# The order of the engines' steps in the first half of a two-part transformer kernel, written out anew

## The reference

```python
q, k, v = (out @ W[l] + b[l] for each of Wq, Wk, Wv)      # 16 heads of 16
Qf, Kf = favor(q), favor(k)     # [exp(u - h), exp(-u - h)], u = x @ omega, h = |x|^2 / 2
a = causal_linear_attention(Qf, Kf, v)   # running sums of Kf and of Kf v, num / den
h = layer_norm(out + a @ Wo[l] + bo[l])
out = layer_norm(h + relu(h @ W1[l] + bf1[l]) @ W2[l] + bf2[l])
```

## Time and profile before

| | |
|---|---|
| median of 3 runs | 2771.56 us (2768.94 to 2773.91) |
| the profiled execution's own time | 2766.34 us |
| its span in the profile | 2764.5 us |
| TensorE, VectorE, ScalarE, GpSimd busy | 95%, 81%, 55%, 53% |
| mean granted TensorE clock | 0.99 |
| chunks' passes of the first half in the span | chunk 0 from 20 us on, the last to about 1360 us |

### The profile page before, as it was taken

The page is one execution under the profiler, slowest core; times in us unless marked ns, Lnnn a source line. Parts: engine busy times, 40 slices in busy tenths (PEclk is TensorE's granted clock), DMA queues, the critical chain, the costliest instruction groups (busy, mean ns, idle before and its releaser), DMA issues.

```text
span 2764.5 us, 61451 instructions
## 1 busy us (share of the span) xinstructions
PE 2632.8 (95%) x21416; PEld 2141.0 (77%) x21416; DVE 2228.9 (81%) x5246; ACT 1516.8 (55%) x3106; POOL 1457.5 (53%) x1406
## 2 busy tenths in 40 slices
PE   6799999999999999999988899999999999999997
PEld 4578878778878887787776688888878778788876
DVE  7678877787677777888899988888888888888875
ACT  3454445444554455444435766777756666666661
POOL 2344344443343445444566766665666666676653
PEclk9999999999999999999999999999999999999999
DMA  3100000010000000000111100000100100101001
GB/s 101 28 9 9 17 2 17 9 38 2 1 1 7 19 26 16 21 17 24 45 46 47 32 10 17 14 17 14 32 29 26 34 16 29 32 29 32 18 26 44
DMA packets 77731, 65.63 MB, mean 24 GB/s; under 512 B 15394, under 2 KB 72698, under 8 KB 77434
## 3 DMA queue, kind: packets, MB, share of 16 engines
q1 hardware_dynamic: 77434, 61.70, 7.4%
HBM read 49.10 MB, written 12.58 MB: 22 GB/s over the span
## 4 chain that ended last, share of the span: by engine, by line
PE 58%; DVE 21%; ACT 10%; issue 8%; POOL 2%; DMA 0%; SPq 0%; DVEq 0%; ACTq 0%; POOLq 0%
PE PS L273 49%; DVE U L1575 3%; PE PS L778 3%; DVE X L1448 2%; DVE ZC L1646 2%; ACT U L1069 2%; ACT U L1070 2%; ACT U L1071 2%; DVE ST L1429 2%; ACT U L1072 1%; DVE Z L1440 1%; ACT FB L1096 1%; PE PS L731 1%; PE PS L740 1%; DVE Z L1528 1%
## 5 line engine op out<-in xcount | busy, mean ns | idle before, releaser
L1251 ACT ACTIVATE PR<-PS,SM 128x256 f32<-128x256 f32 (+1 forms) x512 | 279.4, 555 | 101.9 <-DVE SM L1767 100.4
L1096 ACT ACTIVATE FB<-PS,BC 128x512 f32<-128x512 f32 x192 | 132.4, 689 | 293.2 <-PE PS L273 290.7
L2159 POOL TENSOR_TENSOR RL<-FB,RH 128x512 fp32r<-128x512 f32 x96 | 124.1, 1293 | 277.2 <-DVE RH L1553 277.2
L1575 DVE TENSOR_TENSOR U<-PS,CST 128x512 f32<-128x512 f32 x384 | 236.4, 677 | 24.1 <-PE PS L273 24.1
L1762 DVE CUSTOM_DVE_ANT_0 PS<-PS,MSK 128x256 f32<-128x256 f32 (+1 forms) x512 | 202.6, 436 | 46.6 <-PE PS L273 45.3
L1104 ACT COPY NUM<-PS 128x256 f32<-128x256 f32 x96 | 35.8, 373 | 353.7 <-DVE TMP L1567 304.1
L273 PE MATMUL PS<-W2H,RH 128*128 128x256 f32 x768 | 222.6, 290 | 4.4 <-DVE RL L1556 3.8
L1553 DVE CAST RH<-FB 128x512 fp32r<-128x512 f32 x192 | 87.8, 457 | 171.2 <-ACT FB L1096 167.6
L2284 POOL TENSOR_TENSOR SM<-SM,COL 128x8 f32<-128x8 f32 x128 | 215.0, 1679 | 10.7
L273 PE MATMUL PS<-W2H,RL 128*128 128x256 f32 x768 | 215.8, 281 | 0.0
L273 PE MATMUL PS<-W2L,RH 128*128 128x256 f32 x768 | 215.3, 280 | 0.0
(11 more groups left out here) (266 smaller groups left out, 8995.1 us busy)
## 6 DMA issues: line engine op xcount, KB each, us to landing
PX<-in_L_attn_x SPq DMA_DIRECT2D x16, 512.0 KB, 4.0
TB<-in_k_rot SPq DMA_DIRECT2D x64, 128.0 KB, 2.1
SG<-in_L_attn_W SPq DMA_DIRECT2D x24, 256.0 KB, 2.7
xp_scratch<-PX SPq DMA_DIRECT2D x8, 512.0 KB, 2.9
xs_scratch<-X SPq DMA_DIRECT2D x64, 64.0 KB, 1.5
ZS<-xs_scratch SPq DMA_DIRECT2D x16, 256.0 KB, 2.9
GG<-xp_scratch SPq DMA_DIRECT2D x7, 512.0 KB, 3.7
out<-GG SPq DMA_DIRECT2D x7, 512.0 KB, 3.7
```

Source lines behind the costliest of these rows:

```text
L1096: e.activation(FB[:, hb % 2, :], PS[:, 5, :], ACT.Relu, bias=BC[:, l % 2, 4 + hb:5 + hb]).then_inc(*a_re.up(n, hb))
L1251: t = e.activation(PR[:, par, 256 * i + lo:256 * i + hi], PS[:, 3 + par, 256 * i + lo:256 * i + hi], ACT.Exp, bias=S[:, 40 + 2 * g + i:41 ...
L1575: e.tensor_tensor(heads(U[:, u % 6, :], 4), heads(PS[:, g, :], 4), bcast(CM, 4), ALU.mult).then_inc(*d_mk.up(n, u))
L2159: e.tensor_tensor(RL[:, r, :], FB[:, 0, :], RH[:, r, :].bitcast(F), ALU.subtract).then_inc(*p_rl.up(n, hb))
```

## The change

No product, mask or norm is added or left out. Four things change.

1. **Laps 2 to 23** get a new order on all four engines. On TensorE the four `favor` stand in one run; `down` 0 and 1 stand ahead of them, `down` 2 to 7 among scores and sums and at the end, three of them behind `scores(n, 3)`; `scores(n, 0)` stands ahead of `key_sums`. VectorE's norms are cut into statistics (`_s`) and centring (`_c`): the first norm's centring lies between `state(n, 0)` and `masks(n, 1)`, its scaling ahead of `masks(n, 3)`. GpSimd's `key_state(n, 0)` lies ahead of `low_hidden(m, 4)`. Each step stays in the lap in which it was.
2. **Laps 0 and 1** and what stands ahead of them are written out step by step. Two modulation products stand ahead of `turn_x(0)`, four among chunk 0's `values` and `favor`, the last two in banks 5 and 6. The splits of the first twelve weight pieces, the gates' rows and the prologues of chunks 2 and 3 have new places.
3. ScalarE copies all six modulation products and adds the 1 in the same step (an activation with bias `ONE`); VectorE's copy and three additions are gone.
4. `k_col`, `k_cst` and the three other constants have semaphores of their own; `k_col` is sent third, the modulation's weights ahead of x, `load_columns(0)` ahead of the last three constants. Waits that stood in the loops stand in the steps' functions.

The new order of TensorE in the opening and in the laps, then ScalarE's, VectorE's (opening's begin and laps) and GpSimd's laps:

```diff
-    MODS = [(0, 0, 4), (1, 0, 5), (0, 1, 6), (1, 1, 7), (0, 2, 0), (1, 2, 1)]
+    MODS = [(0, 0, 4), (1, 0, 5), (0, 1, 6), (1, 1, 7), (0, 2, 5), (1, 2, 6)]
...
+        modulate(0)
+        modulate(1)
         turn_x(0)
+        proj(0, 0)
+        proj(0, 1)
+        proj(0, 2)
+        proj(0, 3)
+        values(0, 0)
+        modulate(2)
+        values(0, 1)
+        modulate(3)
+        favor(0, 0, 2)
+        modulate(4)
+        favor(0, 1, 3)
+        modulate(5)
+        favor(0, 2, 0)
+        favor(0, 3, 1)
...
+        for n in range(2, 24):
+            w, m = n - 1, n - 2
+            up(m, 0)
+            spread(w)
+            up(m, 1)
+            proj(n, 0)
+            proj(n, 1)
+            up(m, 2)
+            proj(n, 2)
+            proj(n, 3)
+            values(n, 0)
+            values(n, 1)
+            down(m, 0)
+            down(m, 1)
+            favor(n, 0, 2)
+            favor(n, 1, 3)
+            favor(n, 2, 0)
+            favor(n, 3, 1)
+            up(m, 3)
+            attn_out(w, 0)
+            attn_out(w, 1)
+            turn_k(n, 0)
+            turn_k(n, 1)
+            up(m, 4)
+            scores(n, 0)
+            key_sums(n)
+            up(m, 5)
+            down(m, 2)
+            sums(n, 0)
+            scores(n, 1)
+            down(m, 3)
+            up(m, 6)
+            sums(n, 1)
+            scores(n, 2)
+            up(m, 7)
+            down(m, 4)
+            sums(n, 2)
+            scores(n, 3)
+            down(m, 5)
+            down(m, 6)
+            down(m, 7)
+            turn_h(w)
+            if n < 23: turn_x(n + 1)
+            sums(n, 3)
...
+            if j == 0:
+                e.activation(MOD[:, b, D:2 * D], PS[:, bank, 256:512], ACT.Identity, bias=ONE)
+                t = e.copy(MOD[:, b, 0:D], PS[:, bank, 0:256])
...
+        for n in range(2, 24):
+            w, m = n - 1, n - 2
+            numerators(w, 3)
+            relu(m, 0)
+            relu(m, 1)
+            operands(n, 0)
+            operands(n, 1)
+            operands(n, 2)
+            operands(n, 3)
+            attention(w, 0)
+            attention(w, 1)
+            relu(m, 2)
+            features(n, 0, 2)
+            features(n, 1, 3)
+            features(n, 2, 0)
+            relu(m, 3)
+            features(n, 3, 1)
+            keep_rows(n, 0)
+            keep_rows(n, 1)
+            relu(m, 4)
+            relu(m, 5)
+            numerators(n, 0)
+            relu(m, 6)
+            relu(m, 7)
+            numerators(n, 1)
+            numerators(n, 2)
+            high_mid(w, 0)
+            high_mid(w, 1)
+            if n < 23: high_row(n + 1, 0)
+            if n < 23: high_row(n + 1, 1)
...
+        clear_values()
+        silu()
         prologue(0)
+        modulate_a(0)
+        modulate_b(0)
         split(0)
         split(1)
+        lower(0, 0, 2, 0, a_x, d_x)
+        lower(0, 1, 3, 0, a_x, d_x)
         split(2)
         prologue(1)
+        split(3)
+        add_bv(0, 0)
         modulate_a(1)
+        split(4)
         modulate_b(1)
+        add_bv(0, 1)
+        running(0, 0)
+        running(0, 1)
+        prologue(2)
+        carry(0)
+        split(5)
+        split(6)
+        masks(0, 0)
+        normaliser(0)
+        state(0, 0)
+        masks(0, 1)
...
+        for n in range(2, 24):
+            w, m, z = n - 1, n - 2, n - 3
+            scale_num(w, 0)
+            scale_num(w, 1)
+            rounded(m, 0)
+            if z >= 0: add_down(z)
+            if z >= 0: norm2_s(z)
             splits(n, "a")
+            rounded(m, 1)
+            if z >= 0: norm2_c(z)
+            add_bv(n, 0)
             splits(n, "v")
+            add_bv(n, 1)
+            if z >= 0: norm2_b(z)
+            running(n, 0)
+            rounded(m, 2)
+            running(n, 1)
+            carry(n)
+            rounded(m, 3)
+            add_wo(w)
+            norm1_s(w)
+            rounded(m, 4)
+            masks(n, 0)
+            normaliser(n)
+            rounded(m, 5)
+            state(n, 0)
+            norm1_c(w)
+            masks(n, 1)
+            rounded(m, 6)
+            if z in CH3: norm3_s(z)
+            if n < 6: prologue(n + 2)
             splits(n, "m0")
+            state(n, 1)
             splits(n, "m1")
+            masks(n, 2)
+            rounded(m, 7)
+            state(n, 2)
+            norm1_b(w)
+            masks(n, 3)
+            if z in CH3: norm3_c(z)
+            if n < 6: modulate_a(n + 2)
+            lower(w, 0, 0, 1, a_h, d_h)
+            lower(w, 1, 1, 1, a_h, d_h)
+            if n < 23: lower(n + 1, 0, 2, 0, a_x, d_x)
+            if n < 23: lower(n + 1, 1, 3, 0, a_x, d_x)
+            state(n, 3)
+            if n < 6: modulate_b(n + 2)
+            if z in CH3: norm3_b(z)
             splits(n, "m2")
...
+        for n in range(2, 24):
+            w, m, z = n - 1, n - 2, n - 3
+            if n == 19: gate_rows(0)
+            if z in CH3: add_bias(z)
+            if n in (2, 11): features_of(1 if n == 2 else 2)
+            add_bf2(m)
+            if z >= 0: rsqrt(("2", z))
+            low_hidden(m, 0)
             splits(n, "a")
+            if n == 19: gate_rows(1)
+            low_attention(w, 0)
+            low_attention(w, 1)
+            low_hidden(m, 2)
+            scale_queries(n, 0)
+            scale_queries(n, 1)
+            key_state(n, 0)
+            low_hidden(m, 4)
+            add_bo(n)
+            splits(n, "m0")
+            rsqrt(("1", w))
+            key_state(n, 1)
             splits(n, "v")
+            low_hidden(m, 6)
             splits(n, "m1")
+            if z in CH3: rsqrt(("3", z))
+            key_state(n, 2)
+            if n < 6: rsqrt(("p", n + 2))
+            key_state(n, 3)
             splits(n, "m2")
...
+        e.dma_start(COL[:, :], ins["k_col"]).then_inc(*s_col.up())
```

More of the change, by code:

```diff
@@ L480, in scores @@
         def scores(n, j):
+            if j == 0:
+                for i in range(2):
+                    e.wait_ge(*a_kt.at(n, i))
+                    if n > 0:
+                        e.wait_ge(*d_z.at(n - 1, i))
+                    else:
+                        e.wait_ge(*a_fe.at(n, i))
             for m in range(2):
@@ L538, in up @@
                     e.wait_ge(*d_h.at(n, k))
+            if n == 0 and hb == 0:
+                e.wait_ge(*a_mod.at(5))
             if hb or n:
@@ new lines, in _ @@
+        proj(0, 0)
[12 more added lines that the diff above has]
+        favor(0, 3, 1)
+        turn_k(0, 0)
+        turn_k(0, 1)
+        scores(0, 0)
+        key_sums(0)
+        scores(0, 1)
+        sums(0, 0)
+        sums(0, 1)
+        scores(0, 2)
+        sums(0, 2)
+        scores(0, 3)
@@ new lines, in _ @@
+        turn_x(1)
+        sums(0, 3)
+        spread(0)
+        proj(1, 0)
+        proj(1, 1)
+        proj(1, 2)
+        proj(1, 3)
+        values(1, 0)
+        values(1, 1)
+        favor(1, 0, 2)
+        favor(1, 1, 3)
+        favor(1, 2, 0)
+        attn_out(0, 0)
+        attn_out(0, 1)
+        favor(1, 3, 1)
+        turn_k(1, 0)
+        turn_k(1, 1)
+        scores(1, 0)
+        key_sums(1)
+        scores(1, 1)
+        sums(1, 0)
+        sums(1, 1)
+        scores(1, 2)
+        sums(1, 2)
@@ new lines, in _ @@
+        scores(1, 3)
+        sums(1, 3)
+        turn_x(2)
+        turn_h(0)
+        for n in range(2, 24):
[42 more added lines that the diff above has]
+            sums(n, 3)
@@ new lines, in _ @@
+        add_bv(0, 1)
[9 more added lines that the diff above has]
+        masks(0, 1)
+        state(0, 1)
+        masks(0, 2)
+        state(0, 2)
+        masks(0, 3)
+        split(7)
+        lower(1, 0, 2, 0, a_x, d_x)
+        lower(1, 1, 3, 0, a_x, d_x)
+        state(0, 3)
+        scale_num(0, 0)
+        scale_num(0, 1)
+        modulate_a(2)
+        split(8)
@@ new lines, in _ @@
+        modulate_b(2)
+        gate_steps(0)
+        add_bv(1, 0)
+        add_bv(1, 1)
+        split(9)
+        split(10)
+        gate_steps(1)
+        running(1, 0)
+        running(1, 1)
+        split(11)
+        carry(1)
+        add_wo(0)
+        norm1_a(0)
+        masks(1, 0)
+        normaliser(1)
+        masks(1, 1)
+        state(1, 0)
+        prologue(3)
+        state(1, 1)
+        masks(1, 2)
+        norm1_b(0)
+        state(1, 2)
+        masks(1, 3)
+        modulate_a(3)
```

575 lines of the change are left out of this document (223 added, 352 removed).

## The result

The changed kernel takes 2795.63 us (median of 4 runs, 2788.70 to 2801.93), the kernel before on the same chip 2772.73 (4 runs): a ratio of 1.009, 95% interval 1.0077 to 1.0103. It is 0.9% slower. The forecast was 2728 us, with a range from 2712 to 2755; "slower" had a chance of 0.05.

A forecast was written before the change was run, and what follows sets the result against it. It took TensorE, busy 95% of the span, to bound the kernel, counted from start to start. Opening 13 plus laps 28 made 41 us off 2,766.3 (2,725.3) or the median (2,730.6), so 2,728 us; range 2,712 to 2,755.

The forecast's parts named there:

- The lap's own time: Laps 2 to 23: TensorE's shortest start-to-start times sum to 54.7 us a lap in the new order, 0.25 less.
- The pairs: New TensorE neighbours in the laps: scores after up 1.09 us, key_sums after scores 0.70, up after down 1.26.
- The frame: Time along a lap, counted from the end of sums(n-1, 3), on which the new order's steps were placed.
- The lap's waits: Laps 2 to 23: waits of 1.36 us a lap fall to 0.35, giving laps of 55.0 us, 28 us less over 22.
- The recorded sign of being wrong: In the laps: over 55.6 us each, with idle before sums(n, 1) on VectorE's masks.
- Rival 1: Laps: waits move instead of going, VectorE stretching beside GpSimd; laps give 5 to 10 us, 2,753 us; chance 0.19.
- Rival 3: Laps: GpSimd's low_hidden(m, 4) behind key_state(n, 0) delays relu(m, 6) and up(m, 7); slower, 2,775 us; chance 0.05.
- Rival 4: Whole kernel: both gains, opening and laps, fail by half and more, within 0.2%, 2,768 us; chance 0.04.
- The opening: Before the full laps, to up(0, 0): earlier starts in chunks 0 and 1 gain 13 us, bounds 8 and 18.
- rival 2: Opening: a lower granted clock takes its gain; half speed in both chunks costs 5 to 10 us, 2,736 us; chance 0.11.
- The ring: Chunk 0: each tile's masks (2.5 us), scores (1.3) and sums in turn, from scores(0, 0) at 41.2 to turn_x(1) at 60.3.
- my chain of handovers: Opening: some 60 handovers between engines, each possibly slipping by tenths, leading to up(0, 0) near 111 us against 125.89.

The follow-up runs named there:

- d1: a2 with VectorE's modulate_b and norm3_b moved behind the next lap's scale_num: 2738.95 us, ratio 0.9878 to the kernel before.
- a1: Changed kernel with VectorE's norm1_c moved behind masks(n, 1): 2755.60 us, ratio 0.9945 to the kernel before.
- a2: Changed kernel with GpSimd's low_hidden(m, 4) and add_bo(n) put back ahead of key_state(n, 0), VectorE untouched: 2759.39 us, ratio 0.9957 to the kernel before.
- e1: Changed kernel with GpSimd's add_bo cut to 8 of each 256 columns, orders and waits kept: 2773.72 us, ratio 1.001 to the kernel before.
- c1: Changed kernel with only VectorE's modulate_b and norm3_b moved behind the next lap's scale_num: 2776.83 us, ratio 1.0029 to the kernel before.
- a5: Changed kernel's new opening with laps 2 to 23 in the old order on all four engines: 2770.39 us, ratio 1.0001 to the kernel before.
- a4: Changed kernel with opening and laps 0 and 1 in the old order; new laps, DMA order and ScalarE copies kept: 2792.73 us, ratio 1.0078.
- g1: d1 with features_of(0) ahead of split(3) and chunk 1's rsqrt, modulation products out from between feature products: 2736.41 us, ratio 0.987; repeated unchanged 2733.39 us.
- a3: Changed kernel with GpSimd's add_bf2 back ahead of key_state(n, 3) at the lap's end: 2799.98 us, ratio 1.0103 to the kernel before.

## Why the prediction was wrong

**The lap's own time: right.** The pairs that I had estimated at 1.09, 0.70 and 1.26 measured 1.10, 0.68 and 1.26 at their shortest in the changed kernel (the first is 1.27 or more in most laps, with the wait of 0.2 us in it). Once the two waits are cured, 21 laps take 1154.8 us in d1, 55.0 each, which is the lap forecast. The gain of some 27 us was there. The frame held as well: from the end of `sums(n-1, 3)`, `masks(n, 1)` ended at 38.5 in lap 12, to the tenth as forecast, and `masks(n, 3)` at 50.6 for 50.5.

**The lap's waits: this is the step that failed.** The prediction had "`masks(n, 1)` now stands behind `norm1_c` and ends at 38.5 ... slack near 0". It took `norm1_c` at the 1.7 us of an undisturbed step, and let the engines meet through semaphores only. But GpSimd's `key_state(n, 0)`, moved ahead of `low_hidden(m, 4)` and `add_bo(n)`, is released by the very `state(n, 0)` that releases `norm1_c`. The passes of the one engine and the instructions of the other take turns: 4.21 us, masks 2.7 late (41.2 in the frame in lap 13), 2.15 of waiting ahead of `sums(n, 1)` in 17 laps. a1 and a2 show it from either side, e1 shows that it is the length of GpSimd's instruction that counts. The recorded sign of being wrong, laps over 55.6 with idle before `sums(n, 1)` on VectorE's masks, is what came. The second place was not looked at at all: `modulate_b` and `norm3_b`, at the lap's end ahead of `scale_num`, beside `add_bf2` and `add_bias`, which the change had moved to the lap's start; c1 and d1 show that `scale_num` behind them is what costs, and the rows of lap 21 what holds them up. Against d1 the changed kernel loses 46.1 us in these 21 laps; the miss there is 46.

**Rival 1 was the mechanism, mis-sized.** It named VectorE's passes stretching beside GpSimd and `masks(n, 1)` behind `norm1_c`, yet said that the laps would still give 5 to 10 us. The row that would have priced it was in hand: `modulate_b(0)` at 3.0 us for 1.7. Each held pass costs up to one GpSimd instruction, 1.5 us here, and the three held passes 2.5; with a slack near 0 and 17 laps that is some 40 us (36.5 measured), not 20. **Rival 3** asked the right question of GpSimd's queue, who stands behind `key_state(n, 0)`, but followed only the semaphore to `relu(m, 6)`, where nothing came late. The queue did cost, by holding VectorE up and not through a semaphore. "Slower" came true by another way than the one that was given 0.05. Rival 4 had both gains fail and nothing lost; the laps lost.

**The opening: forecast 13, measured nothing** (a5: 1.0001; a4 against the changed kernel: 2.9 us better with the old one). The first steps held, and were better than forecast: `proj(0, 0)` at 17.1 (18.5 forecast, 22.3 before). Three terms failed. First, the four remaining products were put "into gaps" at nothing; two of them stand between feature products, 1.9 us each, and with the feature map late at 33.20 `scores(0, 0)` started at 45.8, not 41.2. g1 gives that back (41.1). Second, the clock: the changed kernel ran at 0.50 (1.2 GHz) from 44 to 60 us, where the kernel before had 0.89 and 0.79 in its two profiles, though from 20 to 44 us no pause of TensorE was over 1.16 us:

```profile
44.00:60.00 16.00, 14.12 (x124) 10.56 (x127) 6.45 (x11) 1.19 (x3) 4.84 (x4) 0.50 0.10 34
```

Its repeat had 0.59 there. Ten of the executions have this opening unchanged; eight of them ran this stretch at 0.50 to 0.67, but a1 and a3 at 0.89. So the lower clock is frequent there but does not belong to the order. What it costs can be read from them. These are the stretches from `scores(0, 0)` to `turn_x(1)`, with the same 196 matmuls, in the changed kernel and in a1:

```profile
45.80:68.60 22.80, 19.13 (x196) 13.86 (x197) 11.79 (x21) 1.12 (x3) 4.49 (x5) 0.67 0.07 24
```

```profile
46.40:65.70 19.30, 15.31 (x196) 10.48 (x197) 11.78 (x21) 1.12 (x3) 4.91 (x5) 0.91 0.09 28
```

22.8 us at 0.67 and 19.3 at 0.91, where 19.1 was forecast; a3 took 19.9, the other eight 22.1 to 22.8. The ring was rightly forecast for the higher clock, and the clock took some 3 us of the gain: that is rival 2, in chunk 0. Third, chunk 1: from `proj(1, 0)` to `up(0, 0)` 53.3 us for 45.4 forecast, 49.8 before. Even g1's repeat, at a clock of 0.93, needs 51.3 (70.5 to 121.8). Its first and second masks come as forecast, 26.0 and 29.7 us behind `proj(1, 0)`; the third come 9.4 us behind the second (6.8 forecast), and `up(0, 0)` starts 7.5 us behind the last masks (4.0 forecast). These two steps are the 6 us by which my chain of handovers was too short; no run tried what lengthens them.

**The rest of the program: forecast unchanged.** It came out 6.4 us longer in this table, which counts lap 23 with it. Lap 23's own two waits are 4.2 us ahead of `proj(23, 0)` and 2.2 ahead of `sums(23, 1)`. The kernel before itself gave 1459.7 and 1467.4, so nothing beyond these two can be told from scatter.

## What to carry to other kernels

Before moving an elementwise pass, list what the neighbour engine will run at that moment; for VectorE and GpSimd a pass with two SBUF inputs is to be priced at up to its own time plus the GpSimd instructions queued for the same release (1.66 us became 4.21 and 5.28 here). Keep such passes, and everything that GpSimd has in store, away from the stretch between a product and the mask or copy that TensorE waits for; behind it the same pass cost nothing (a1, d1). A quick test after a reordering is the page's part 1: (nearly) equal instruction counts with more busy time on both engines were the sign of the collision here.

## What the runs showed of the hardware

- The collision is exclusive and goes instruction by instruction: passes of 0.48 us lasted 0.95, 1.51 and 1.50, each ending 0.28 us behind one of GpSimd's. A GpSimd instruction of 1.30 us took 1.47 in it. Masks, which read one operand from PSUM, took 669 to 693 ns in all 384 cases.
- Cutting a GpSimd instruction's size doesn't cut its time in proportion: `add_bo` cut from 512 to 16 elements a partition went from 1.47 to 0.40 us, not to a thirtieth. Its smallest, 128x4 elements recorded with 1.0 to 1.5 us, held none of the 53 passes that lay inside it.
- Executions of one kernel differ by up to 5 us in the opening, at granted clocks that differ in single stretches (0.68 and 0.89 from 92 to 108 us), while its laps, at full clock, repeat within 1.6 us. One stretch of 196 matmuls took 22.8 us at 0.67 and 19.3 at 0.91. A change to an opening of 120 us is told by its early steps in two or three profiles, not by the median alone.
